# Two graph layers on one core: the edge plan in rows of one superblock a partition, spread between the batches of the relation table, and gathers that read their indices in place

## The chip, the cores and the metric

One core of one Trainium2 chip. The metric is the device time of one execution in microseconds. The median of three runs is given, and the profile is of a fourth execution.

## What is computed

12,500 nodes with 64 features, 400,000 edges sorted by destination, 16 edge types. Two layers, each with layer norm, ReLU and a residual:

```python
edge_index = jnp.stack([src, dst])
h = jnp.maximum(_layernorm(x, axis=-1), 0.0)
# layer 0: out[dst] += h[src] @ weight[edge_type]
x = x + _L0_gnn_ref(h, L0_gnn_weight, src, dst, edge_type_16)
h = jnp.maximum(_layernorm(x, axis=-1), 0.0)
# layer 1: mean of h[src] over the edges of dst, @ W_l + b_l, + h @ W_r,
#          + (edge_attr @ W_e + b_e) of the last edge of dst
x = x + _L1_gnn_ref(h, edge_index, edge_attr_16, ...)
```

## The kernel before

**Tiling.** P is 128. Nodes lie in NT = 98 tiles of 128, in NB = 14 batches of TB = 7 tiles. Edges lie in S = 125 superblocks of 128 x K, K = 25; a superblock is NG = 5 groups of G = 5 columns. A *slot* is one group, so there are SLOTS = 625 slots.

**Stage 1, loads and plan (lines 686 to 848 and 1225 to 1306).** SP loads `dst_f` (destinations, 125 partitions of 3,200, line 736), `idx` (sources in the layout partition, superblock, column, so in runs of 100 bytes, line 737), `x_sb` (rows of 256 bytes, node tile t in column t, line 738) and the weights. ACT loads `dst_i` (runs of 100 bytes), `nxt` (the destination of each column's next edge, single elements, lines 834 and 836) and the types. VectorE makes one-hots of every 16th destination in 40 steps (`hist_onehots`, line 1247), which TensorE sums to a histogram (line 1003). VectorE packs source and destination into one word (lines 1259 and 1261); ACT writes the words to DRAM (842) and copies them within DRAM to `runs`, 25,000 overlapping rows of 128 words (844 and 846). Then come checks and ends of the superblocks (lines 1275 to 1302), which end in `flag` and `s_plan`. GpSimd makes row numbers `idx * 16 + type` (701, 703). All engines are one straight line of waits here.

**Stage 2, the table.** For each batch VectorE normalises 7 tiles in six steps (`norm_step`, lines 642 to 672), TensorE turns them (1053), ACT applies ReLU (855), TensorE multiplies each tile by all 16 weights (1043, into two alternating pairs of PSUM banks), ACT and VectorE each evict one half (864, 1320) and SP stores 512 KB a tile to `rel_table` (755), 4 KB a partition. Batch n + 1 is normalised between the evictions of batch n - 1. TensorE waits for the weights before its first batch (1031, 1032).

**Stage 3, the slots.** GpSimd issues 5 indirect DMAs a slot (`gather_group`, lines 471 to 477), one row of 64 floats for each partition, with indices in `istage`. ACT copies those 5 columns of indices there (`stage_group`, 489 to 491) once the product of five slots before has freed the group (`free`), and writes the edge attributes into `msg` (893). VectorE makes one-hots of the destinations, TensorE multiplies (`product_group`, 485). The rest of the three engines' time goes to counts of edges for each pair of node tiles (lines 1069, 884, 1386 and 1387; stored by `store_counts`), which stand for layer 1's gathers and are multiplied by its features (1127). `runs_at` lists the slots after which GpSimd also gathers 128 rows of `runs` (714); its first is slot 5, and VectorE takes them from its own slot 6 on (`make_keys`, 1348). SP works through a fixed list by slot: `load_attr` at c % 5 == 1 (waits for `attr_used`), `store_counts`, `load_room`, and at slot 622 `load_piece` of the first three pieces of counts. Every instruction waits in its engine's order.

**Stage 4, the tail.** Counts come back in 106 pieces through 7 places (787) and are multiplied (1143) and evicted (1535, 1539).

## Time and profile before

| | us |
|---|---|
| median of 3 runs (lowest, highest) | 4618.67 (4602.07, 4619.43) |
| the profiled execution's own time | 4602.55 |
| its span | 4600.7 |
| busy: PE, DVE, ACT, POOL | 3003.2, 3500.4, 2121.8, 3103.8 |
| mean granted TensorE clock | 0.822 of full |

The span is that of the instructions; the execution's own time is 1.85 us more. Busy times are sums over the whole span and say little here, since the stages have different limits. The page also gives the chain of work that ended last, the costliest groups of instructions, and the DMA issues; the trace gives timelines, waits and busy time by stretch. POOL is GpSimd, DVE VectorE, ACT ScalarE, PE TensorE, SP the queue engine; a trailing q marks the queue's own instructions.

### The profile page before, as it was taken

To read this page: it belongs to the slowest core of one execution; us is meant where nothing else is said; L and a number is where in the kernel's file an instruction comes from. 1 tells how busy PE (TensorE), PEld (TensorE's weight loads), DVE (VectorE), ACT (ScalarE), POOL (GpSimd) and SP (SyncE) were. 2 spreads that over 40 slices of the span, in tenths; PEclk is the share of its full clock that TensorE was granted. 3 is DMA by queue.
4 is the path that set the end of the run, shared out by engine and by line. 5 is a ranking of instruction groups with operands and counts; after the bars stand their busy time and mean duration, and the time that the engine had idled before them with its cause. 6 is when DMAs were issued, how large, how long until landed. Compare 5 with 4: busy or idle time off the path is not lost.

```text
span 4600.7 us, 83711 instructions
## 1 busy us (share of the span) xinstructions
PE 3003.2 (65%) x23324; PEld 2426.3 (53%) x23325; DVE 3500.4 (76%) x17508; ACT 2121.8 (46%) x7155; POOL 3103.8 (67%) x3190
## 2 busy tenths in 40 slices
PE   1464555555565666565676677766777777777799
PEld 1123444444444544454565555655666666666689
DVE  5564778778788877887888888887888888888833
ACT  0243455545455554554545455454554554545400
POOL 1017777777777777777777777777777777777700
PEclk9985767767777777787787788878988989989999
DMA  9872333333323433242342433423423333332379
GB/s 101 262 307 61 116 92 116 114 110 110 101 85 109 136 120 113 92 131 76 100 142 87 126 117 91 124 74 112 121 82 111 113 94 107 109 89 76 111 286 383
DMA packets 315349, 575.64 MB, mean 125 GB/s; under 512 B 124155, under 2 KB 227259, under 8 KB 303515
## 3 DMA queue, kind: packets, MB, share of 16 engines
q1 hardware_dynamic: 135494, 443.69, 26.9%
q0 software_dynamic: 101568, 105.81, 11.4%
q10 hardware_dynamic: 77842, 20.86, 3.6%
q8 instruction: 198, 3.24, 0.3%
q14 instruction: 247, 2.02, 0.1%
HBM read 334.10 MB, written 248.81 MB: 127 GB/s over the span
## 4 chain that ended last, share of the span: by engine, by line
POOL 59%; issue 20%; PE 9%; DMA 6%; ACT 2%; DVE 2%; ACTq 1%; another core or an unknown queue 1%; POOLq 0%; SPq 0%; DVEq 0%
POOL msg L475 58%; DMA msg<-rel_table,istage 5%; PE ps L1143 4%; PE ps L1043 2%; PE ps L485 2%; ACT arena L884 2%; POOL wrel L714 1%; ACTq L846 1%; DVE onehot L1247 1%; DMA arena<-counts 1%; PE ps L1127 1%; DMA arena<-in_dst 0%; PE ps L1069 0%; DVE arena L670 0%
## 5 line engine op out<-in xcount | busy, mean ns | idle before, releaser
L475 POOL DMA_INDIRECT msg<-rel_table,istage x3125 | 3040.3, 973 | 953.7 <-issue 939.9
L884 ACT CAST arena<-ps 128x392 bf16<-128x392 f32 x3136 | 1326.5, 511 | 1945.7 <-PE ps L1069 1930.8
L485 PE MATMUL ps<-onehot,msg 128*81 128x128 f32 x6250 | 1083.5, 336 | 1124.7 <-DMA msg<-rel_table,istage 1082.3
L485 PEld LDWEIGHTS ps<-onehot,msg 128*81 128x81 f32 x6250 | 925.3, 192 | 1225.2 <-DMA msg<-rel_table,istage 1099.7
L1387 DVE TENSOR_SCALAR batch<-iota_h,wrel 128x196 bf16<-128x196 bf16 x4312 | 1248.2, 294 | 0.0
L1386 DVE TENSOR_SCALAR batch<-iota_h,wrel 128x128 bf16<-128x128 bf16 x4312 | 1173.5, 275 | 0.0
L503 DVE TENSOR_SCALAR onehot<-iota_w,arena 128x128 f32<-128x128 f32 x3125 | 684.9, 299 | 544.0 <-PE ps L485 542.6
L1069 PE MATMUL ps<-batch 128*128 128x196 bf16 x4312 | 761.6, 287 | 186.6 <-DVE batch L1387 88.9
L893 ACT ACTIVATE msg<-attr,arena 128x16 f32<-128x16 f32 x3125 | 693.6, 317 | 4.5 <-DMA attr<-in_edge_attr 4.4
L1127 PE MATMUL ps<-arena 128*128 128x192 bf16 x7238 | 690.0, 254 | 0.0
L1127 PEld LDWEIGHTS ps<-arena 128*128 128x128 bf16 x7238 | 636.6, 102 | 7.4 <-issue 0.3
L1069 PEld LDWEIGHTS ps<-batch 128*128 128x128 bf16 x4312 | 396.9, 110 | 446.1 <-DVE batch L1387 212.4
L1387 DVE TENSOR_SCALAR arena<-iota_h,wrel 128x196 bf16<-128x196 bf16 x1960 | 568.5, 294 | 0.0
L1386 DVE TENSOR_SCALAR arena<-iota_h,wrel 128x128 bf16<-128x128 bf16 x1960 | 537.8, 277 | 6.8 <-PE ps L1069 5.9
L1069 PE MATMUL ps<-arena 128*128 128x196 bf16 x1960 | 358.7, 284 | 105.7 <-ACT arena L884 49.3
L1069 PEld LDWEIGHTS ps<-arena 128*128 128x128 bf16 x1960 | 185.5, 109 | 234.2 <-issue 112.7
L1143 PE MATMUL ps<-arena 128*128 128x192 bf16 x2366 | 197.4, 246 | 4.4 <-DMA arena<-counts 3.8
L1143 PEld LDWEIGHTS ps<-arena 128*128 128x128 bf16 x2366 | 195.1, 98 | 5.8 <-issue 5.7
L1399 DVE TENSOR_TENSOR arena<-arena,ps 81x128 f32 x125 | 35.1, 281 | 200.4 <-PE ps L485 195.2
L491 ACT COPY istage<-arena 128x5 int32<-128x5 int32 x625 | 135.7, 217 | 69.9 <-PE ps L485 61.3
L708 POOL MEMSET msg<- 128x25 f32 x1 | 0.1, 140 | 221.8 <-DMA rel_table<-arena 221.8
L1535 DVE TENSOR_REDUCE batch<-ps 128x64 f32<-128x192 f32 x98 | 35.0, 357 | 114.4 <-PE ps L1143 114.4
(149 smaller groups left out, 1210.9 us busy)
## 6 DMA issues: line engine op xcount, KB each, us to landing
arena<-counts SPq DMA_DIRECT2D x458, 224.0 KB, 4.3
rel_table<-arena SPq DMA_DIRECT2D x98, 512.0 KB, 3.5
msg<-rel_table,istage POOLq DMA_INDIRECT x3125
counts<-arena SPq DMA_DIRECT2D x10, 3136.0 KB
arena<-counts SPq DMA_DIRECT2D x28, 896.0 KB, 11.9
attr<-in_edge_attr SPq DMA_DIRECT2D x125, 200.0 KB
counts<-arena SPq DMA_DIRECT2D x8, 2688.0 KB
arena<-counts SPq DMA_DIRECT2D x31, 672.0 KB, 10.8
```

Source lines behind the costliest of these rows:

```text
L475: pool.indirect_dma_start(msg[:, k, 0:D], None, table, bass.IndirectOffsetOnAxis(ap=istage[:, k:k + 1].bitcast(U32), axis=0)).then_inc(got ...
L485: mm = pe.matmul(ps[0:rows, bank, 0:WIN], msg[:, k, 0:rows], onehot[:, k, :], start=(k == 0), stop=(k == K - 1))
L491: copy(istage[:, g * G:g * G + G], slots(idx, s, g)).then_inc(ly["staged"], 1)
L503: ins = nc.vector.tensor_scalar(onehot[:, k, :], iota_w[:, :], where, None, ALU.is_equal)
L884: nc.scalar.copy(cblk[:, h, :, u * WU * WD:(u + 1) * WU * WD].rearrange("p t (w d) -> p w t d", d=WD), unit_cols(b, u).rearrange("p w (t d ...
L893: ins = nc.scalar.activation(msg[:, k, D + 1:M0], attr[:, k, :], ACT.Copy, scale=mark)
L1043: mm = pe.matmul(bank, hTs[q * D:(q + 1) * D, h, t, :], wrel_flat[q * D:(q + 1) * D, half], start=True, stop=True)
L1069: mm = pe.matmul(unit_cols(b, u)[:, w, :], oh_lo[i], oh_hi[i], start=True, stop=True)
L1127: mm = pe.matmul(mult_bank(k), weights, y3d[:, t, :], start=(t == m["t0"]), stop=(t == m["t1"] - 1))
L1143: mm = pe.matmul(tail_bank(b), places[i % PLACES].rearrange("p (t n) -> p t n", n=P)[:, t - t0, :], y3d[:, t, :], start=(t == done[b]), st ...
L1386: nc.vector.tensor_scalar(oh_lo[i], iota_h[:, 0:P], kcol[:, 1, c:c + 1], None, ALU.is_equal)
L1387: ins = nc.vector.tensor_scalar(oh_hi[i], iota_h[:, :], kcol[:, 0, c:c + 1], None, ALU.is_equal)
```

## The change

- **Layout of the plan.** Destinations, sources and types are loaded one superblock of 3,200 edges a partition (`dst_n`, `src_n`, `typ_n`, 125 partitions; the first two with 112 edges of the next superblock, so that `nxt`, `dst_f`, `dst_i`, `idx` and `typ_i` are not loaded). Row numbers, last marks and places in the window are made there and turned by TensorE into the old layout: 75 transposes in 21 turns of up to 4, each copied out by ACT (`turn_edges`, `take_turn`).
- **x for the table.** Each partition takes 98 consecutive nodes (127 partitions of 25,088 bytes, and one of 13,824); table rows are addressed to match. The tile layout is loaded again in 7 parts by SP at slots 8 to 14 for stage 3.
- **Order.** The 40 histogram steps (5 a batch) and the plan (`plan_step(n)`) are laid between the batches; only the first 5 histogram steps come before them. ACT evicts both halves of tiles 1, 3 and 5 of a batch. All batches are unrolled.
- **runs** are stored from SBUF by SP at slots 0 to 7, 16 partitions each (200 rows of 512 bytes a partition), instead of over DRAM by ACT. The first gather of them moves from slot 5 to slot 9 and waits for all these stores.
- **Gathers** wait for `free` themselves and read their index column in `idx`; `istage` is not used in this path. Waits on `staged` become waits on the landing of the gathers.

```diff
+    NAT, HALO = P * K, P - GRAIN
+    WIDE = NAT + HALO
+    HELD = NT - (NN - N)
+    ACT_ROWS = (1, 3, 5)
+    HIST_EACH = 5
+    TURN_K = 4
+    turns = [(v, k, min(k + TURN_K, K)) for v in range(3) for k in range(0, K, TURN_K)]
+    TURN_POINTS = [(n, j) for n in (2, 3) for j in range(3)] + [(4, 0), (8, 1), (8, 2)] + [
+        (n, j) for n in range(9, 13) for j in range(3)]
+    turn_at_point = {point: i for i, point in enumerate(TURN_POINTS)}
+    assert len(turns) == len(TURN_POINTS)
+    ROWS_AT, ROWS_AFTER = 7, 7
+    RUN_PARTS, X_PARTS = 8, 7
...
-        packed = rel.bitcast(I32)
...
-        nxt = sb("nxt", [P, S], I32)
...
-        t0v = table0.rearrange("(t p r) d -> p t (r d)", p=P, r=R)
+        t0v = table0.rearrange("(p t r) d -> p t (r d)", p=P, r=R)
...
+        def dve_rows(i):
+            return i // TB * (TB - len(ACT_ROWS)) + sum(t not in ACT_ROWS for t in range(i % TB))
+        def x_tiles(j):
+            return j * (NT // X_PARTS), min((j + 1) * (NT // X_PARTS), FULL)
...
-            pool.wait_ge(s_pack, 2)
-            nc.gpsimd.tensor_single_scalar(idx, idx, R, ALU.mult).then_inc(s_rowno, 1)
-            pool.wait_ge(s_rowno, 1)
-            nc.gpsimd.tensor_tensor(idx, idx, typ_i, ALU.add).then_inc(s_rowno, 1)
-            pool.wait_ge(s_rowno, 2)
-            pool.wait_ge(s_edges, 3)
...
-                    gather_group(pool, LY[0], got[0], table0, c // NG, c % NG)
+                    pool.wait_ge(LY[0]["free"], c + 1)
+                    pool.nop(nofuse=True)
+                    for k in range(c % NG * G, c % NG * G + G):
+                        pool.indirect_dma_start(
+                            msg[:, k, 0:D], None, table0,
+                            bass.IndirectOffsetOnAxis(ap=idx[:, c // NG, k:k + 1].bitcast(U32),
+                                                      axis=0)).then_inc(got[0][c % NG], 16)
                     if c == runs_at[0]:
-                        pool.wait_ge(s_runs, 32)
+                        pool.wait_ge(s_runs, (RUN_PARTS + 1) * 16)
...
-            sp.dma_start(dst_f, dst.rearrange("(p c g) -> p c g", p=FP, g=GRAIN)).then_inc(s_dstf, 16)
-            sp.dma_start(idx, edges(src)).then_inc(s_idx, 16)
-            sp.dma_start(x_sb[:, 0:FULL], xv).then_inc(s_x, 16)
+            sp.wait_ge(s_xfill, 1)
+            sp.dma_start(x_flat[0:P - 1], x[0:(P - 1) * NT].rearrange("(p t) d -> p (t d)", t=NT)).then_inc(s_x, 16)
+            sp.dma_start(x_flat[P - 1:P, 0:HELD * D], x[(P - 1) * NT:N].rearrange("(p t) d -> p (t d)", p=1)).then_inc(s_x, 16)
...
-            sp.wait_ge(s_xfill, 1)
-            sp.dma_start(x_sb[0:PART, FULL], x[FULL * P:N, :]).then_inc(s_x, 16)
...
+            sp.wait_ge(s_turned, len(turns))
...
-                    sp.wait_ge(LY[0]["staged"], SLOTS)
+                    sp.wait_ge(got[0][NG - 1], S * 16 * G)
...
+            def store_runs(j):
+                p0, p1, most = j * (P // RUN_PARTS), min((j + 1) * (P // RUN_PARTS), S - 1), NAT // GRAIN
+                part = packed_n[p0:p1]
+                sp.dma_start(runs[p0 * most:p1 * most, :].rearrange("(p r) e -> p r e", r=most),
+                             bass.AP(part.tensor, part.offset, [part.ap[0], [GRAIN, most], [1, P]])).then_inc(s_runs, 16)
...
+                    if 0 <= c < RUN_PARTS:
+                        store_runs(c)
+                    if RUN_PARTS <= c < RUN_PARTS + X_PARTS:
+                        load_x(sp, c - RUN_PARTS)
...
-            act.dma_start(dst_i, edges(dst)).then_inc(s_dst, 16)
-            act.wait_ge(s_nfill, 1)
-            act.dma_start(nxt[:, 0:S - 1], dst[K:K + (S - 1) * P * K].rearrange("(s p k) -> p s k", p=P, k=K)[:, :, 0:1]
-                          .rearrange("p s k -> p (s k)"), allow_slow_non_contiguous=True).then_inc(s_nxt, 16)
-            act.dma_start(nxt[0:P - 1, S - 1:S], dst[K + (S - 1) * P * K:E].rearrange("(p k) -> p k", k=K)[:, 0:1],
-                          allow_slow_non_contiguous=True).then_inc(s_nxt, 16)
-            act.dma_start(typ_i, edges(edge_type)).then_inc(s_typ, 16)
-            act.wait_ge(s_pack, 2)
-            act.dma_start(edges(ends), packed).then_inc(s_ends_out, 16)
-            act.wait_ge(s_ends_out, 16)
-            act.dma_start(runs[0:MAXRUN, :],
-                          bass.AP(ends.tensor, ends.offset, [[GRAIN, MAXRUN], [1, P]])).then_inc(s_runs, 16)
-            act.dma_start(runs[MAXRUN:MAXRUN + 1, :], ends[E - P:E].rearrange("(r e) -> r e", r=1)).then_inc(s_runs, 16)
+            act.wait_ge(s_nfill, 2)
+            for v, o, done_sem in ((dst, dst_n, s_dst), (src, src_n, s_idx)):
+                act.dma_start(o[0:S - 1], bass.AP(v.tensor, v.offset, [[NAT, S - 1], [1, WIDE]])).then_inc(done_sem, 16)
+                act.dma_start(o[S - 1:S, 0:NAT], v[(S - 1) * NAT:E].rearrange("(s e) -> s e", s=1)).then_inc(done_sem, 16)
+            act.dma_start(typ_n.bitcast(I32), edge_type.rearrange("(s e) -> s e", s=S)).then_inc(s_typ, 16)
...
+            def take_turn(n, j):
+                if (n, j) not in turn_at_point:
+                    return
+                i = turn_at_point[n, j]
+                v, k0, k1 = turns[i]
+                act.wait_ge(s_turn, i + 1)
+                if v > 0:
+                    act.wait_ge(s_hmm, FR // HC)
+                nc.scalar.copy((idx, last, rel)[v][:, :, k0:k1].rearrange("p s k -> p k s"),
+                               ps[:, 3, 0:(k1 - k0) * S].rearrange("p (k s) -> p k s", s=S)).then_inc(s_turned, 1)
...
+                        if t in ACT_ROWS:
+                            nc.scalar.copy(tbuf[:, t], ps[:, bank:bank + 2, :]).then_inc(FA["actout"], 1)
+                        else:
+                            nc.scalar.copy(tbuf[:, t, 0], ps[:, bank, :]).then_inc(FA["actout"], 1)
...
-                    stage_group(LY[0], 0, 0, c, act, nc.scalar.copy)
...
+            def turn_edges(n, j):
+                if (n, j) not in turn_at_point:
+                    return
+                i = turn_at_point[n, j]
+                v, k0, k1 = turns[i]
+                pe.wait_ge(s_edges, v + 1)
+                if i >= 1:
+                    pe.wait_ge(s_turned, i)
+                if i == ROWS_AFTER:
+                    pe.wait_ge(s_rowsc, 1)
+                pe.nop(nofuse=True)
+                for k in range(k0, k1):
+                    mm = pe.transpose(ps[:, 3, (k - k0) * S:(k - k0 + 1) * S], by_edge[v][:, k, :], ident[0:S, 0:S])
+                mm.then_inc(s_turn, 1)
...
+                turn_edges(n, 0)
+                if n >= 1:
+                    rel_rows(n - 1, 1 - h, n)
+                for c in range(n * HIST_EACH, min((n + 1) * HIST_EACH, FR // HC)):
+                    hist_step(c)
+            for n in range(NB):
+                table_batch(n, n % 2)
+            rel_rows(NB - 1, 1, NB)
...
-            def hist_onehots(c, q):
-                if n_from(c, 2):
-                    dve.wait_ge(s_hmm, c - 1)
-                for r, lo, hi in ((0, 0, P), (1, P, P + NP)):
-                    ins = nc.vector.tensor_tensor(
-                        hoh[:, q, :, lo:hi], iota_h[0:FP, 0:hi - lo].unsqueeze(1).broadcast_to([FP, HC, hi - lo]),
-                        fcol[:, r, bass.ds(c * HC, HC)].unsqueeze(2).broadcast_to([FP, HC, hi - lo]), ALU.is_equal)
-                ins.then_inc(s_hoh, 1)
-            hist_onehots(0, 0)
-            hist_onehots(1, 1)
-            with dve.Fori(1, FR // HC // 2) as i:
-                for q in range(2):
...
+            def hist_onehots(n):
+                for c in range(n * HIST_EACH, min((n + 1) * HIST_EACH, FR // HC)):
+                    if c >= HOHS:
...
+            def plan_step(n):
+                here, after = dst_n[:, 0:NAT], dst_n[:, 1:NAT + 1]
+                if n == 1:
+                    dve.wait_ge(s_idx, 32)
+                    dve.wait_ge(s_typ, 16)
+                    nc.vector.scalar_tensor_tensor(out=idx_n, in0=src_n[:, 0:NAT], scalar=float(R), in1=typ_n.bitcast(I32),
+                                                   op0=ALU.mult, op1=ALU.add).then_inc(s_edges, 1)
+                if n == 2:
+                    dve.wait_ge(s_edges, 1)
+                    nc.vector.tensor_single_scalar(packed_n, src_n, NODE_BITS, ALU.arith_shift_left).then_inc(s_pack, 1)
+                    dve.wait_ge(s_pack, 1)
+                    nc.vector.tensor_tensor(packed_n, packed_n, dst_n, ALU.bitwise_or).then_inc(s_pack, 1)
+                if n == 3:
+                    link(nc.vector.tensor_tensor(last_n, after, here, ALU.is_lt))
+                if n == 4:
+                    link(nc.vector.tensor_reduce(bad[0:S, 1:2], last_n, AX, ALU.max))
+                if n == 5:
+                    link(nc.vector.tensor_reduce(col[0:S, 0:1], here, AX, ALU.min))
+                if n == 6:
+                    link(nc.vector.tensor_reduce(col[0:S, 1:2], here, AX, ALU.max))
...
+                if n == 7:
+                    nc.vector.tensor_tensor(last_n, here, after, ALU.not_equal).then_inc(s_edges, 1)
+                    dve.wait_ge(s_pack, 2)
+                    dve.wait_ge(s_edges, 2)
+                    nc.vector.tensor_scalar(rel_n, here, col[0:S, 0:1], None, ALU.subtract).then_inc(s_edges, 1)
...
+            hist_onehots(0)
...
+                    if m >= 0 and t not in ACT_ROWS:
...
+            for n in range(NB):
+                plan_step(n)
+                hist_onehots(n + 1)
+                take_rows(n - 1, 1 - n % 2, n, n % 2)
...
+                if n == 0:
+                    dve.wait_ge(s_x2, (X_PARTS + 1) * 16)
```

## Rows read from the trace of the kernel before

**Rows 1.** The page: the chain that ended last, shares of the span.

```profile
POOL 59%; issue 20%; PE 9%; DMA 6%; ACT 2%; DVE 2%; ACTq 1%; another core or an unknown queue 1%; POOLq 0%; SPq 0%; DVEq 0%
```

**Rows 2.** Page, costliest groups: line, engine, form, count | busy, mean ns | idle, releaser.

```profile
L475 POOL DMA_INDIRECT msg<-rel_table,istage x3125 | 3040.3, 973 | 953.7 <-issue 939.9
...
L491 ACT COPY istage<-arena 128x5 int32<-128x5 int32 x625 | 135.7, 217 | 69.9 <-PE ps L485 61.3
```

**Rows 3.** Waits of POOL: who for whom, total us, times, longest.

```profile
POOL msg L475 <- ACT istage L491: 13.8, 41, 1.6
```

**Rows 4.** Timeline, end of the table and first gathers: start us, us, engine line, operands.

```profile
309.65 0.59 ACT L864 COPY arena<-ps 128x512 f32<-128x512 f32 x1 [0.56 <-PE ps L1043]
...
319.10 0.14 POOL L708 MEMSET msg<- 128x25 f32 x1 [221.83 <-DMA rel_table<-arena]
...
320.87 4.29 POOL L475 DMA_INDIRECT msg<-rel_table,istage  x1 [1.63 <-ACT istage L491]
```

**Rows 5.** Timeline, the first 180 us: loads, histogram, plan, first transposes.

```profile
0.78 0.40 SPq L736 DMA_DIRECT2D arena<-in_dst  x1
...
2.75 37.02 SPq L738 DMA_DIRECT2D x_sb<-in_x  x1
...
21.27 0.33 DVE L1237 TENSOR_SCALAR arena<-arena 125x200 int32<-125x200 int32 x1 [17.97 <-DMA arena<-in_dst]
...
22.41 42.45 DVE L1247 TENSOR_TENSOR onehot<-iota_h,arena 125x640 bf16<-125x640 bf16 x80
...
64.76 1.79 DVE L1259 TENSOR_SCALAR arena<-arena 128x3125 int32<-128x3125 int32 x1
...
66.59 3.42 DVE L1261 TENSOR_TENSOR arena<-arena 128x3125 int32<-128x3125 int32 x1
...
76.49 3.41 DVE L1276 TENSOR_REDUCE attr<-arena 128x125 f32<-128x3125 int32 x1
...
123.89 42.51 ACTq L846 DMA_DIRECT2D edge_runs<-edge_ends  x1
...
169.72 1.73 PE L1053 MATMUL ps<-ident,arena 128*128 128x128 f32 x7 [34.84 <-DVE arena L670]
```

**Rows 6.** Timeline, one batch of the table.

```profile
239.15 0.95 PE L1053 MATMUL ps<-ident,arena 128*128 128x128 f32 x7 [0.99 <-DVE arena L670]
...
240.04 7.51 PE L1043 MATMUL ps<-wrel,onehot 64*128 64x512 f32 x28
...
241.31 0.69 DVE L1320 COPY arena<-ps 128x512 f32<-128x512 f32 x1 [1.17 <-PE ps L1043]
241.91 0.62 DVE L652 SCALAR_TENSOR_TENSOR batch<-stat,x_sb 128x448 f32<-128x448 f32 x1
...
247.31 1.08 DVE L670 TENSOR_TENSOR arena<-batch,stat 128x896 f32<-128x896 f32 x1
```

**Rows 7.** Stretches: busy time (x instructions) by engine, PEclk, DMA share, GB/s.

```profile
200.00:300.00 100.00, 87.47 (x375) 32.95 (x373) 80.62 (x136) 55.37 (x96) 0.00 (x0) 1.00 0.98 392
...
4376.00:4420.00 44.00, 38.36 (x422) 37.98 (x423) 9.13 (x21) 4.26 (x10) 0.46 (x1) 0.88 0.42 145
...
4450.00:4500.00 50.00, 50.00 (x609) 50.00 (x607) 18.00 (x56) 0.00 (x0) 0.00 (x0) 1.00 1.03 408
```

**Rows 8.** DMA issues: operands, queue, count, KB each, us from issue to landing.

```profile
edge_runs<-edge_ends ACTq DMA_DIRECT2D x1, 12496.0 KB, 45.4
...
arena<-in_dst SPq DMA_DIRECT2D x1, 1562.5 KB
```

**Rows 9.** Timeline, last slots: staging, loads of counts, last gather, first tail product.

```profile
4350.98 0.25 ACT L491 COPY istage<-arena 128x5 int32<-128x5 int32 x1
...
4352.28 1.29 SPq L787 DMA_DIRECT2D arena<-counts  x3
...
4375.51 0.94 POOL L475 DMA_INDIRECT msg<-rel_table,istage  x1 [0.30 <-issue]
...
4392.20 1.40 PE L1143 MATMUL ps<-arena 128*128 128x192 bf16 x15
```

More of the change, by code:

```diff
@@ L76, in gnn_two_layers @@
     turn_at = [unit_slot(2 * m - 1, UB - 1) - 1 for m in range(NP)]
-    runs_at = [NG] + [unit_slot(2 * m - 2, RUNS_AT) for m in range(1, NP)]
+    runs_at = [RUN_PARTS + 1] + [unit_slot(2 * m - 2, RUNS_AT) for m in range(1, NP)]
     taken = set(turn_at) | {c + 1 for c in turn_at}
@@ L296, in gnn_two_layers @@
         s_pack = sem("s_pack")
-        s_ends_out = sem("s_ends_out")
         s_runs = sem("s_runs")
@@ L788, in load_piece @@
                              counts_of(b, t0, t1)).then_inc(cloaded[i % PLACES], 16)
+            def store_runs(j):
[3 more added lines that the diff above has]
+                             bass.AP(part.tensor, part.offset, [part.ap[0], [GRAIN, most], [1, P]])).then_inc(s_runs, 16)
+                if p1 == S - 1:
+                    part = packed_n[p1:S]
+                    sp.dma_start(runs[p1 * most:MAXRUN + 1, :].rearrange("(p r) e -> p r e", p=1),
+                                 bass.AP(part.tensor, part.offset, [part.ap[0], [GRAIN, MAXRUN + 1 - p1 * most], [1, P]])
+                                 ).then_inc(s_runs, 16)
             def load_room(i):
@@ L817, in _ @@
             with sp.Else():
+                for j in range(X_PARTS):
+                    load_x(sp, j)
                 for_steps(sp, load_attr)
@@ L872, in _ @@
             dense = is_dense(act)
-            act.wait_ge(s_rowno, 2)
-            act.wait_ge(s_edges, 3)
+            act.wait_ge(s_turned, len(turns))
             def write_unit(b, u):
                 h = b % 2
+                if u == 0 and b == 0:
+                    act.wait_ge(s_runs, (RUN_PARTS + 1) * 16)
                 if u == 0 and b >= 2:
@@ L888, in attr_group @@
             def attr_group(s, g):
+                act.wait_ge(LY[0]["free"], s * NG + (g + 1))
                 if g == 0:
@@ L998, in _, with hist_step @@
         def _(pe):
-            def hist_step(c, q, first=False, end=False):
+            def hist_step(c):
                 pe.wait_ge(s_hoh, c + 1)
                 for k in range(HC):
-                    mm = pe.matmul(ps[:, 7, 0:NP], hoh[:, q, k, 0:P], hoh[:, q, k, P:P + NP],
-                                   start=(k == 0 and first), stop=(k == HC - 1 and end))
+                    mm = pe.matmul(ps[:, 2, 0:NP], hoh[:, c % HOHS, k, 0:P], hoh[:, c % HOHS, k, P:P + NP],
+                                   start=(k == 0 and c == 0), stop=(k == HC - 1 and c == FR // HC - 1))
@@ L1005, in hist_step @@
                 mm.then_inc(s_hmm, 1)
-            HS = FR // HC
-            hist_step(0, 0, first=True)
-            hist_step(1, 1)
-            with pe.Fori(1, HS // 2 - 1) as i:
-                for q in range(2):
-                    hist_step(i * 2 + q, q)
-            hist_step(HS - 2, 0)
-            hist_step(HS - 1, 1, end=True)
-            pe.wait_ge(s_hist, 1)
-            pe.matmul(ps[0:NP, 6, 0:P], hist[:, :], ones[:, :], start=True, stop=True).then_inc(s_tot, 1)
-            pe.wait_ge(s_totc, 1)
@@ L1045, in rel_rows @@
                     mm.then_inc(FA["rows"], 1)
+                    if t == 2:
+                        turn_edges(n, 1)
+                    if t == 5:
+                        turn_edges(n, 2)
             def table_batch(n, h):
+                plan_step(n)
                 pe.wait_ge(FA["norm"], n + 1)
[L1049 to L1050 removed]
+                if n >= 1:
+                    pe.wait_ge(FA["relu"], n)
                 pe.nop(nofuse=True)
                 for t in range(TB):
[L1053 removed]
+                    mm = pe.transpose(tile_cols(0, 0, P)[:, t, :], twice[:, h, t].rearrange("p q d -> p (q d)"),
                                       ident[:, :])
                 mm.then_inc(FA["hT"], 1)
[L1056 to L1059 removed]
+                turn_edges(n, 0)
+                if n >= 1:
+                    rel_rows(n - 1, 1 - h, n)
+                for c in range(n * HIST_EACH, min((n + 1) * HIST_EACH, FR // HC)):
+                    hist_step(c)
+            for n in range(NB):
+                table_batch(n, n % 2)
+            rel_rows(NB - 1, 1, NB)
+            pe.wait_ge(s_plan, 1)
             dense = is_dense(pe)
```

252 lines of the change are left out of this document (131 added, 121 removed).

## The prediction

> **What bounds the kernel now.** I read the chain of waits first, since busy shares over the whole span mix four stages. It gives POOL 59% and "issue" 20% [rows 1]. The costliest groups say what that is: 3,125 indirect DMAs of 973 ns with 0.3 us between them [rows 2], so (3040.3 + 953.7) / 3125 = 1.278 us each and 3,994 us of a 4,601 us span, on one engine that never pauses longer. The waits of POOL show what the indices' staging costs it: 13.8 us in 41 waits [rows 3], of which 41 x 0.3 = 12.3 are the gap that stands before every gather anyway. The slots are thus bound by POOL's own time for a gather, and no other engine matters there unless it stops POOL.
>
> What is left is ahead of the first gather and behind the last. The first gather starts at 320.87, right after the last row of the table has landed (319.10) [rows 4]. Within that, the first transposes of the table start at 169.72 [rows 5], and its last tile is evicted at about 310 [rows 4]: 141.5 us of table after 169.7 us of loads and plan. The tail runs from the last gather at 4375.51 [rows 9] to 4600.7. The change works on the first 320 us.
>
> **Gathers without staging.** 625 copies of 217 ns leave ACT [rows 2], which is not the bound. POOL gains at most 13.8 - 12.3 = 1.5 us. The index column is read with the same 128 accesses; nothing in the trace prices another base address, so between -20 ns and +20 ns a gather (60 us either way) I take 0, because the gathers of the shown rows take 0.94 us whichever column of the staging tile they read [rows 9]. With the staging wait gone POOL waits for `free`, which is what ACT waited for: at the end of the slots the staging of the last slot was done at 4350.98 while POOL came to its last gather at 4375.51 [rows 9], so POOL trails its permission by 20 us and sees neither. Term: -2.
>
> **When x is there.** This decides the case. The table now starts with x and nothing of the plan except five histogram steps. The kernel before has one load with an odd number of rows: `dst_f`, 125 rows of 12,800 bytes, issued at 0.78 [rows 5]; VectorE, which waits for it, starts at 21.27. That is 1562.5 KB [rows 8] in 20.4 us, 78 GB/s, where transfers of 128 rows reach 408 GB/s [rows 7], or 408 / 16 = 25.5 GB/s for each of 16 DMA engines. My reading: whole rows are dealt in equal shares, so the number of engines must divide the number of rows. 128 gives 16, 125 gives 5 (at most 127 GB/s, and 78 beside the other loads), 124 gives 4, and 127, a prime, gives one. The new x is 127 rows of 25,088 bytes, 3.19 MB: 3.19 / 25.5 = 125 us on one engine. The new loads of destinations and sources (124 rows, 4 engines) and types (125 rows, 5) put 0.42 + 0.42 + 0.32 = 1.16 MB on each of their first engines, 46 us. They are issued in the same microsecond as x. If they meet on its engine x lands at 0.8 + 125 + 46 = 172 us, otherwise at 126. I take 172, since the load of 125 rows got 78 of 127 GB/s, so it did share its engines with the queue beside it.
>
> The Trainium skill, "DMA: Bandwidth & Descriptors", section "Why a DMA increments its semaphore by 16 and not by 1", states this as a rule: the largest number up to 16 that divides the outermost dims, taken from the lowest-numbered engines, with 127 partitions as its example of one engine. By it x lands at 172, at 126 never; no row here shows a transfer of 127 long rows.
>
> From x to the first transposes are the six steps of `norm_step`: four of 0.62, ACT 0.3, reciprocal 0.2, the last 1.08 [rows 6], 4.4 us. So 176.5 against 169.7. Term: +7. The 40 histogram steps (42.45 us) and the plan [rows 5] would have fitted into this wait, and so would all work on sources and destinations; but VectorE stands at its wait for x, and all of it is queued behind.
>
> **The table with the plan in it.** A batch took 9.4 us before: TensorE 0.95 for transposes and 7.51 for products [rows 6], VectorE 80.6 and ACT 55.4 in 100 us, and DMA share 0.98 at 392 GB/s [rows 7]. Added on VectorE, in order: five histogram steps of 42.45 / 40 = 1.06, 5.3 us a batch for n = 0 to 6; plan steps over 3,200 columns, which cost 3.5 for two inputs or a reduction and 1.8 for one input (3.42, 3.41 and 1.79 for 3,125 [rows 5]): 3.5, 5.3, 3.5, 3.5, 3.5, 4.5, 6.2 and 0.9 for n = 1 to 8. They stand ahead of the evictions of their batch. TensorE has two pairs of banks, so after two tiles it waits for VectorE: nothing covers the rest of this time. From the end of the plan step the batch needs about 8.0: VectorE's first norm step and eviction (0.62 + 0.69), five more tiles at 1.13, an eviction by ACT of 1,024 columns (twice 0.58 [rows 4]) in the chain, the last eviction. So n = 0: 9.9 (histogram and norm only); n = 1 to 7: 16.8, 18.6, 16.8, 16.8, 16.8, 17.8, 14.2; n = 8: 9. The 21 turns have four transposes each, 4 x 0.137 [rows 6], and a round trip to ACT's copy of 500 columns, about 1.2 us on TensorE when it stands between tiles; three in each of batches 9 to 12 make these 13, and those of batches 2 and 8 add 2 each. The last batch and its rows take 9.5 + 8. Sum: 9.9 + 117.8 + 9 + 4 + 52 + 17.5 = 210, with 2 for the small steps of n = 9 to 12: 212, against 141.5. Term: +70.5, with -25 (if half of VectorE's part hides) and +20 (if transposes over a stride of 100 bytes or the unrolled code cost more) as bounds. ACT has some 8 us of work in such a batch and is covered. The stores of table rows have a longer pitch in DRAM; they now need 3.67 MB in 17 us instead of 9.4, so even at half their rate they are hidden.
>
> **The stores of runs.** They leave the first part (where `runs` took 42.5 us of issue at 123.89 [rows 5], waited for by ACT's square root) and come beside slots 0 to 7: 12.8 MB in rows of 512 bytes, eight DMAs of 16 partitions. POOL comes to its first gather of runs after 50 gathers, 3.3 + 50 x (0.94 + 0.30) = 66 us from the first one [rows 4, 9], and now waits there for all stores; behind this wait are all later gathers, so it costs one for one. The same bytes took 45.4 us within DRAM [rows 8], 282 GB/s; at the 78 GB/s of the 125-row load they would take 164. From the first value (the same packet size and the same target, so the nearest) parts 0 to 5 are written by 40 us; parts 6 and 7 are issued only after slot 5's attributes, at about 45, and are there at 60 to 75. Term: +8, bounds 0 and +100. The loads of x for stage 3 (3.2 MB, needed at slot 57) and of attributes are small beside that.
>
> **The tail.** SP now waits at slot 622 for the landing of the last gathers, about 4381.6, instead of loading three pieces at 4352.28. Their first product was at 4392.20 [rows 9]; 4.5 MB take 11 us, and DMA was used at 42% up to 4420 [rows 7], so most is absorbed. Term: +2, bounds 0 and +10.
>
> **Sum.** -2 + 7 + 70.5 + 8 + 2 = +85.5 on the profiled execution's 4602.6, thus 4688. Two of the three runs shown lie 16 to 17 above that execution and one equals it, so I say **4695**. This case's own range, from its bounds, is 4640 to 4735. Chance 0.42.
>
> **Rivals.**
> *Stores through a narrow side.* If 16 neighbouring partitions are reached through a quarter of the paths, the stores run at 4 x 25.5 = 102 GB/s and take 125 us; they begin 4 us before the first gather, so POOL waits from 66 to 121 or later, 58 us instead of 8: 4745, range 4725 to 4790. It decides as soon as the stores need over 70 us, 183 GB/s. For it: 78 GB/s of the 125-row load shows that row placement can cost; against: nothing here shows it for 16 rows. Chance 0.34. The Trainium skill, "SBUF — State Buffer", section "Door 1: The DMA port swizzle", states it: partitions 0 to 15 reach 4 of 16 ports, measured 104 GB/s at 1 MiB. By that figure the stores take an estimated 123 us.
> *x spread over all engines* (faster). Then all 8 MB land in 20 us at 408 GB/s; VectorE has its first destinations by about 12, and transposes start near 27 instead of 169.7: -143 + 70.5 + 8 = -64: 4540 to 4560, or 4600 with narrow stores. It decides where x lands before about 87 us (172 less the 85 of the sum), 37 GB/s. Against it stands 78 GB/s for 125 rows. Chance 0.15.
> *VectorE's new work hides* and the table stays near 150: 4625. Against: two pairs of banks, and 80% of VectorE used already. Chance 0.09.
>
> **How the numbers follow.** A measurement here tells about 0.5%, 23 us. Faster by more: 0.12 (x spread, stores not narrow). Within: 0.10 (x spread with narrow stores 0.03, hidden work 0.07). Slower: 0.78. The range reaches up over the narrow stores and down to the edge of the spread cases, 4605 to 4775; outside are 0.12 below and some 0.06 above.
>
> **What would show it.** Right: in the changed profile VectorE's first reduction of x after a DMA wait of over 100 us; a period of 17 us in batches 1 to 6; POOL's gathers without a change in duration, one wait of POOL for the stores of runs. Wrong: a first transpose before 90 us, or a table of under 180 us. The wait of POOL at its 51st gather separates the first two cases: under 20 us or over 45.

## The result, and the profile after

The changed kernel takes 4746.59 us (median of four runs, 4742.94 to 4748.93); the kernel before, beside it on the same chip, 4613.12 (4602.07 to 4619.43). The ratio is 1.0286 with a 95% interval of 1.0262 to 1.0311. The profiled execution took 4742.94 with a span of 4741.1, 140.4 more than the span before. The direction and the range were right, the case forecast as likeliest was not: 4746.6 lies beyond that case's own end of 4735 and on the rival of the narrow stores (4745). The forecast of 4695 was 82 us of loss, and 133.5 were measured.

The waits of POOL in the changed kernel (who waited for whom: total us, times, longest), which answer to [rows 3]:

```profile
POOL msg L744 <- issue: 926.4, 3031, 3.0
POOL msg L729 <- DMA rel_table<-arena: 394.1, 1, 394.1
POOL wrel L735 <- DMA edge_runs<-arena: 63.0, 1, 63.0
POOL msg L744 <- PE ps L512: 28.6, 94, 0.3
```

One new wait stands there, 63.0 us at the first gather of `runs`. The gathers themselves, from the page's costliest groups, are as in [rows 2]:

```profile
L744 POOL DMA_INDIRECT msg<-rel_table,arena x3125 | 3044.9, 974 | 955.1 <-issue 926.4
```

The start, VectorE's timeline (against [rows 5]): beside twelve short instructions, this is all that VectorE did in the first 177 us.

```profile
61.43 0.33 DVE L1317 TENSOR_SCALAR arena<-arena 125x200 int32<-125x200 int32 x1 [55.81 <-DMA arena<-in_dst]
...
62.56 5.39 DVE L1328 TENSOR_TENSOR arena<-iota_h,arena 125x640 bf16<-125x640 bf16 x10
176.91 0.62 DVE L674 TENSOR_REDUCE stat<-x_sb 128x7 f32<-128x448 f32 x1 [108.97 <-DMA x_sb<-in_x]
```

And stretches of the same execution (start and end, length, busy time of PE, PEld, DVE, ACT and POOL with their instructions, granted clock, DMA share, GB/s; the columns of [rows 7]). The first is the load of x by itself, the next two are batches of the table, and the last is the time in which POOL waits for the stores of `runs`.

```profile
100.00:160.00 60.00, 0.00 (x0) 0.00 (x0) 0.00 (x0) 0.00 (x0) 0.00 (x0) 1.00 0.06 27
...
210.00:231.00 21.00, 11.91 (x62) 5.25 (x61) 16.05 (x22) 8.78 (x12) 0.00 (x0) 0.76 0.44 178
...
332.60:373.00 40.40, 39.17 (x189) 18.45 (x188) 24.97 (x44) 34.25 (x47) 0.00 (x0) 1.00 0.84 342
...
461.00:530.00 69.00, 7.27 (x30) 6.15 (x30) 0.00 (x0) 5.07 (x25) 4.80 (x6) 0.50 0.70 110
```

A DMA share of 0.06 is one engine of sixteen, at 27 GB/s: the x of 127 rows. The next two stretches show the table in its two forms: with the plan in it TensorE works 11.9 of 21 us at a mean clock of 0.76; without it, from 332.6 on, 39.2 of 40.4 at 1.00.

**Where the 140.4 us are.** Each line compares the same two events in the profiles. The last eviction of the table is VectorE's, first in the kernel before and then in the changed one:

```profile
310.51 0.69 DVE L1320 COPY arena<-ps 128x512 f32<-128x512 f32 x1 [0.17 <-PE ps L1043]
...
389.17 0.69 DVE L1415 COPY arena<-ps 128x512 f32<-128x512 f32 x1 [1.50 <-PE ps L1112]
```

| stretch | before | after | difference | predicted |
|---|---|---|---|---|
| start to first transposes of x | 169.72 | 182.80 | +13.1 | +7 |
| to the end of that eviction (311.20, 389.86) | 141.5 | 207.1 | +65.6 | +70.5 |
| to the first gather (320.87, 399.09) | 9.67 | 9.23 | -0.4 | 0 |
| POOL's wait for `runs` | 0 | 63.0 | +63.0 | +8 |
| rest, first to last gather (last at 4375.51, 4520.83) | 4054.6 | 4058.7 | +4.1 | -2 |
| last gather to the end | 225.2 | 220.3 | -4.9 | +2 |
| sum | 4600.7 | 4741.1 | +140.4 | +85.5 |

Of the 55 us by which the sum was short, the stores of `runs` are 55. The errors of the other terms are -6.9 to +6.1 us and add up to nothing, which is luck.

### The profile page after: what moved, and what is told of

It is laid out like the page before. It is cut to its first block, busy times and chain, and to the rows that moved or that the text cites. A ratio compares the mean times of both kernels' runs of the same rounds, so it can differ in the third digit from the quotient of the medians.

```text
span 4741.1 us, 82631 instructions
## 1 busy us (share of the span) xinstructions
PE 3016.7 (64%) x23397; PEld 2436.7 (51%) x23398; DVE 3484.4 (73%) x17468; ACT 2094.7 (44%) x6549; POOL 3094.3 (65%) x3188
## 4 chain that ended last, share of the span: by engine, by line
POOL 53%; issue 17%; PE 13%; DMA 7%; another core or an unknown queue 3%; DVE 3%; SPq 2%; ACT 1%; POOLq 0%; ACTq 0%; DVEq 0%
POOL msg L744 52%; DMA msg<-rel_table,arena 6%; PE ps L512 5%; PE ps L1222 4%; PE ps L1112 2%; SPq L821 2%; PE ps L1206 1%; POOL wrel L735 1%; DVE arena L1328 1%; PE ps L1148 1%; DMA arena<-counts 1%; DMA edge_runs<-arena 1%; SPq L788 0%; DVE batch L1477 0%
## 5 line engine op out<-in xcount | busy, mean ns | idle before, releaser
L744 POOL DMA_INDIRECT msg<-rel_table,arena x3125 | 3044.9, 974 | 955.1 <-issue 926.4
L951 ACT ACTIVATE msg<-attr,arena 128x16 f32<-128x16 f32 x3125 | 679.6, 316 | 94.8 <-DMA attr<-in_edge_attr 52.9
L1112 PE MATMUL ps<-wrel,onehot 64*128 64x512 f32 x392 | 115.7, 708 | 50.9 <-DVE arena L1415 48.0
L1127 PE MATMUL ps<-ident,arena 128*128 128x128 f32 x98 | 15.1, 299 | 189.4 <-DVE arena L697 189.4
```

Of the source, the lines that this page charges most:

```text
L744: pool.indirect_dma_start(msg[:, k, 0:D], None, table0, bass.IndirectOffsetOnAxis(ap=idx[:, c // NG, k:k + 1].bitcast(U32), axis=0)).then_ ...
L951: ins = nc.scalar.activation(msg[:, k, D + 1:M0], attr[:, k, :], ACT.Copy, scale=mark)
L1112: mm = pe.matmul(bank, hTs[q * D:(q + 1) * D, h, t, :], wrel_flat[q * D:(q + 1) * D, half], start=True, stop=True)
```

## The experiments

Where a kernel was timed once, its time is compared with that of the changed kernel's profile (4742.94); where it was timed several times beside the kernel before, the ratio to that kernel is given with its 95% interval. The time of the slots differs from execution to execution for no cause that I know: in the thirteen profiles with the new gathers the stretch from the first gather to the last, less POOL's wait for `runs`, takes 4058.7 to 4081.3 us. A single time is thus good to some 20 us, and I read each step from the events around it.

### x on more engines

The load of x, one of 127 partitions, is cut in two; nothing else is edited.

```diff
-sp.dma_start(x_flat[0:P - 1], ...)
+sp.dma_start(x_flat[0:112], ...)
+sp.dma_start(x_flat[112:127], ...)
```

> The changed kernel with one edit: the load of x in 127 rows is made in two, 112 rows and 15 rows. Theory (the number of DMA engines divides the number of rows, so 127 rows ran on one): 16 and 15 engines carry it, each engine's share of x falls from 3.19 MB to about 0.2 MB, and VectorE's first reduction of x moves from 176.9 us to about 33, where the five histogram steps end; the first batches then wait some 10 us for sources and types, whose 4 and 5 engines still carry 1.16 MB each (until about 58). First gather at about 265 instead of 399, time about 4607. Rival (long rows of 25 KB or the two queues side by side are slow, whatever the number of rows): x stays beyond 150 us and the time within 10 us of 4743.

Measured: 4635.4, a first gather at 291.71 instead of 399.09, 107.4 us earlier. VectorE no longer waits for x at all: its first reduction follows the histogram steps (48.20 to 53.5) directly. It comes at 53.5 and not at 33, since VectorE has its destinations only at 47.07. And the gain was to be some 28 us more. VectorE's and TensorE's timelines say why:

```profile
47.07 0.33 DVE L1318 TENSOR_SCALAR arena<-arena 125x200 int32<-125x200 int32 x1 [41.45 <-DMA arena<-in_dst]
...
53.50 0.61 DVE L674 TENSOR_REDUCE stat<-x_sb 128x7 f32<-128x448 f32 x1
...
79.84 1.73 PE L1128 MATMUL ps<-ident,arena 128*128 128x128 f32 x7 [79.84 <-DMA bl<-in_L_gnn_b_l]
```

VectorE's part was ready at 59 (its last norm step ran 58.04 to 59.13). TensorE waited for the last of the weights, which stand behind x in SP's queue. SP's own rows of this kernel show it held there:

```profile
3.86 0.40 SPq L764 DMA_DIRECT2D x_sb<-in_x  x1
...
17.32 48.61 SPq L770 DMA_DIRECT2D wcomb<-in_L_gnn_W_l  x1
65.98 3.88 SPq L771 DMA_DIRECT2D wcomb<-in_L_gnn_W_r  x1
...
70.75 2.06 SPq L774 DMA_DIRECT2D bl<-in_L_gnn_b_l  x1
```

The issue of one 16 KB weight took 48.6 us. From 20 to 50 us the DMA share was 0.38, some six of the sixteen engines: the loads of destinations, of sources and of types were still under way. The same cut at another place, 124 partitions and 3:

> The same load in 124 rows and 3 rows, a middle dose. Theory: 4 engines, so the first of them carries 31 rows of x (0.78 MB), three small remainders and 1.16 MB of the other loads, together 1.98 MB at 25.5 GB/s = 78 us: VectorE's first reduction of x at about 82 us, first gather at about 305, time about 4648. Rival (no dependence on the number of rows): as the changed kernel, reduction at 177.

Measured: 4674.34. Destinations arrive at 77.01, the reduction of x at 83.44, and TensorE starts at 112.46, again behind the weights. 124 rows, a multiple of 4, are 32.6 us worse at the first transposes than 112 rows, a multiple of 16, with the same bytes in the same number of loads; the first gather is at 323.85, 32.1 later. When x itself landed the trace does not date here: VectorE reads it right behind its histogram steps, which began when the destinations came. The number of rows decides, and the first cause of the late start is settled. My two forecasts were low by 28 and 26 us, each time because I left out what is late next: the weights.

### The stores of runs

The same 12.8 MB stand in the same partitions of SBUF; what is edited is which of them one store takes. First by columns: each of eight stores takes 25 rows of every one of 112 partitions, and one more store takes the 12 partitions that are left.

```diff
-part = packed_n[p0:p1]                  # 16 neighbours, 200 rows of each
+part = packed_n[0:112]                  # 112 partitions, 25 rows of each
```

> The changed kernel with the stores of runs cut by columns instead of by partitions: eight stores of 112 partitions x 25 rows of 512 bytes, one of the 12 partitions left and the last one; as many bytes, as many packets, the same 16 engines. Theory (16 neighbouring partitions are reached through a quarter of the paths): 11.5 MB go at 280 GB/s in 41 us and the 12 partitions take 15, so all are there by about 55 us after the first gather and the wait of POOL falls from 63 us to under 5: about 4682. Rival (packets of 512 bytes out of SBUF, or their issue on SP, are the limit): the wait stays above 50 us.

Measured: 4691.04. POOL does not wait for `runs` at all. The total is 9 us over the 4682 that were expected; the slots took 4071.6 us instead of 4058.7. Then with wider groups of neighbours, in one kernel four parts of 32 partitions and in another two of 64:

```diff
-p0, p1, most = j * (P // RUN_PARTS), min((j + 1) * (P // RUN_PARTS), S - 1), NAT // GRAIN
+p0, p1, most = j * 32, min((j + 1) * 32, S - 1), NAT // GRAIN
```

> The changed kernel, with the stores of runs in 4 parts of 32 neighbouring partitions (slots 0 to 3) instead of 8 of 16; nothing else. Theory A (a group of 16 neighbours reaches a quarter of the paths, 32 reach half): the stores run at up to 204 GB/s instead of 96, 12.8 MB take about 65 to 75 us from 394, so they are there at 460 to 470, when GpSimd arrives (464): its wait falls from 63 to 0 to 12 us, total 4683 to 4695. Rival B (the queue or the 512 byte packets set the rate, not the width; both forms divide by 16): the wait stays near 63 and the total near 4743. Rival C (a fixed cost of each store, which column parts of 112 partitions also had): the wait would halve, total about 4712.

> The changed kernel, with the stores of runs in 2 parts, partitions 0 to 63 and 64 to 123 (slots 0 and 1). Theory A (paths are reached by position, and partition p + 32 lies on the path of p): 64 neighbours are no wider than 32, but the two parts lie on different halves and may run side by side: the wait of GpSimd is 0 to 12, total 4680 to 4695. If they run one after the other, as 4 parts of 32. Rival B (a rate set by the queue or by 512 byte packets): wait near 63, total near 4743. The second part has 60 partitions, so it may be dealt to 15 or 12 engines; a wait of 5 to 20 more is put to that.

Measured: waits of 7.5 and 6.1 us; times 4704.99 and 4691.63. Both waits are what was expected; the first time is 10 above its range, and its slots took longer otherwise (4076.9 from first to last gather less the wait, against 4058.7). These forms also have fewer and larger stores, which a rival could claim. So last the clean one: eight stores of the same size at the same slots, and only other partitions in each. (Their rows in DRAM, one stretch of 1.6 MB a store before, now lie apart; in the parts of 32 they are one stretch, so that this is not what helps.)

```diff
-part = packed_n[p0:p1]
+part = packed_n[j:S - 1:RUN_PARTS]      # j, j + 8, j + 16, ...
```

> The changed kernel with the 8 stores of runs as they are in size and slot, but each takes every eighth partition (j, j + 8, ...: 16 or 15 of them) instead of 16 neighbours. Theory A (the place of the partitions sets the rate): the store runs at twice 96 GB/s or more, it is there when GpSimd comes, wait 0 to 15, total 4680 to 4697. Rival B (16 partitions a store are too few, wherever they lie, or the waits of SP's queue between 8 stores cost the time): wait 45 to 63, total 4725 to 4745.

Measured: 4685.56, a wait of 6.4. POOL's wait in this kernel:

```profile
POOL wrel L735 <- DMA edge_runs<-arena: 6.4, 1, 6.4
```

The stretches of the stores beside the gathers say how fast each form went. First this kernel:

```profile
402.00:461.00 59.00, 19.39 (x80) 16.42 (x80) 5.86 (x27) 8.80 (x40) 44.68 (x48) 0.53 0.90 213
```

the changed kernel in the same stretch:

```profile
406.00:461.00 55.00, 16.16 (x70) 13.71 (x70) 5.68 (x26) 5.51 (x25) 41.59 (x45) 0.53 0.81 135
```

the four parts of 32:

```profile
408.00:461.00 53.00, 19.38 (x80) 16.42 (x80) 5.63 (x26) 5.51 (x25) 40.20 (x43) 0.50 0.90 212
```

the two parts of 64:

```profile
400.00:461.00 61.00, 19.38 (x80) 16.42 (x80) 7.37 (x35) 6.28 (x31) 46.67 (x48) 0.50 0.89 211
```

and the stores by columns, the last third of this time:

```profile
440.00:461.00 21.00, 8.20 (x34) 7.09 (x35) 0.00 (x0) 3.30 (x15) 16.04 (x17) 0.50 1.05 282
```

All of these count gathers and attributes in too. Sixteen neighbours reach 135 GB/s (110 once the gathers stop, at 461), sixteen partitions spread over SBUF 213, 32 neighbours 212, 64 neighbours no more than that, 211. Neither the packets (512 bytes in all), nor the number of stores, nor the number of partitions in one holds the stores at the narrow rate, but the partitions' place; the theory of the narrow side is shown. By columns the rate is 282 with all DMA engines busy (a DMA share of 1.05; from 449.6 on loads of x are counted in too), as much as the copy within DRAM had; whether the packets of 512 bytes set this upper limit was not tried. The Trainium skill, "SBUF — State Buffer", section "Door 1: The DMA port swizzle", has this as a rule: partitions 0 to 15 reach 4 ports of 16, 32 neighbours 8, and 64 no more than 32. The traces agree in all three, as far as rates tell that count other traffic in; the kernel's 12.8 MB in the 133 us from 393.5 to about 527 are 96 GB/s, beside the 104 that this page of the Trainium skill gives. By this rule of the Trainium skill a stride of 8 also reaches 8 ports, as the 213 beside the 212 of 32 neighbours bears out.

What holds POOL in the narrow form is not the whole cost. SP's list, in the changed kernel:

```profile
405.88 65.38 SPq L821 DMA_DIRECT2D edge_runs<-arena  x5
471.30 14.00 SPq L788 DMA_DIRECT2D attr<-in_edge_attr  x1
485.35 14.30 SPq L821 DMA_DIRECT2D edge_runs<-arena  x2
499.70 14.00 SPq L825 DMA_DIRECT2D edge_runs<-arena  x1
```

Each issue takes 13 to 14 us; with every eighth partition the same five take 33.30, 6.7 each, so the time of the issue goes with the rate of the stores. ACT waits 42.19 us for the attributes in between (its row at 490.45). All of it is over before POOL goes on at 527.18, so I count nothing more for it.

### The table and the histogram

All 40 histogram steps ahead of VectorE's wait for x (and TensorE's sums ahead of its wait for the weights), in an otherwise unedited changed kernel:

```diff
-hist_onehots(0)
+for n in range(-(-(FR // HC) // HIST_EACH)):
+    hist_onehots(n)
 dve.wait_ge(s_x, 32)
```

> The changed kernel with all 40 histogram steps ahead of VectorE's wait for x, and their products ahead of TensorE's wait for the weights, where both are idle. Theory (work of VectorE between the batches is covered by nothing, as TensorE stands after two tiles): seven times 5.4 us leave the table and nothing is added ahead of x; first gather 38 us earlier, at about 361, time about 4705. Rival (TensorE's products, 8 us a batch, cover most of it): less than 15 us are gained.

Measured: 4700.14, 42.8 less, with x 2.1 us earlier (174.81) and the first gather 42.4 earlier (356.67).

```profile
180.70 1.73 PE L1129 MATMUL ps<-ident,arena 128*128 128x128 f32 x7 [77.42 <-DVE arena L697]
...
330.53 0.98 PE L1129 MATMUL ps<-ident,arena 128*128 128x128 f32 x7
```

From the first to the last transposes the table takes 149.8 us (180.70 to 330.53) instead of 190.5 (182.80 to 373.27): 40.6 us for 35 steps that occupy VectorE for 37.7 (seven groups of 5.38) and TensorE, whose sums moved with them, for 5.6 (seven of 0.80). At most 2.7 us of the histogram were hidden between the batches, which ends the rival of the hidden work for this part; and in the idle wait for x the histogram was free. What is left, 149.8 against 125.8 in the kernel before (169.72 to 295.56), is 24.0 us for the plan steps and the turns together. They were not moved, and what each of them costs is not shown.

### Gathers without staging

The kernel before with this part alone:

```diff
-gather_group(pool, LY[0], got[0], table0, c // NG, c % NG)
+pool.wait_ge(LY[0]["free"], c + 1)
+for k in range(...):
+    pool.indirect_dma_start(msg[:, k, 0:D], None, table0, bass.IndirectOffsetOnAxis(ap=idx[:, c // NG, k:k + 1] ...
...
-stage_group(LY[0], s, s, g, act, nc.scalar.copy)
```

> The kernel before with one part of the change alone: gathers wait for the free group themselves and read their index column in place, no staging copies on ACT. My term is -2 us of about 4613, so a ratio of 0.9995, same. Rival (the gather reads its indices slower or faster from the big array): 20 ns a gather either way, 60 us, ratio 0.987 or 1.013; the mean gather then is 953 or 993 ns instead of 973.

Measured: 4602.52 against 4607.32, ratio 0.9995 (0.998 to 1.001). POOL's waits of 13.8 for ACT are gone, and 34.4 us of the same 0.3 us gaps are put down to TensorE's `free` instead:

```profile
POOL msg L723 <- issue: 919.3, 3012, 1.6
...
POOL msg L723 <- PE ps L485: 34.4, 113, 0.3
```

919.3 + 34.4 = 953.7, the 953.7 of [rows 2]. The staging cost nothing.

### Both repairs, and beyond

> The changed kernel with both repairs: x loaded as 112 and 15 partitions, and runs stored in 8 column parts of 112 partitions. The two gains measured alone against the changed kernel were 107.5 (4635.4) and 51.9 us (4691.0). Theory: they lie at different places (before the table, after slot 8) and add up: 4742.9 - 107.5 - 51.9 = 4583.5, 0.7% under the kernel before. Rival: the stores of runs meet the attributes in both and only the sum of POOL's wait (54.8 in the first) can go: 4580. Rival: GpSimd, no longer held at slot 8, runs into the loads of x for stage 3 and pays 10 to 20 us back: 4600.

Measured: 4586.29, ratio 0.9936 (0.9915 to 0.9958) against the kernel before. The two gains add up, as the theory had it (4583.5); the first rival (4580) is too near to be told from it.

Then also the loads of destinations, sources and types, cut at partition 112:

```diff
-act.dma_start(o[0:S - 1], ...)
+act.dma_start(o[0:112], ...)
+act.dma_start(o[112:S - 1], ...)
```

> As x_wide_and_runs_by_columns, and the loads of destinations, sources and types split at partition 112 as well. Theory (the first 30 us are bound by how few engines carry these loads): destinations were there at 47.1 and the weights, which TensorE waits for ahead of its first transposes, at 79.8; with all loads on 14 to 16 engines 8 MB at 300 to 400 GB/s are in by 27 to 35 us, and the first transposes start at 35 to 45: 35 to 45 us less than the one before, 4540 to 4550. Rival: the loads' many queue entries hold the weights, which stay last on SP's queue: transposes at 60, 4565.

Measured: 4541.90, ratio 0.9856 (0.9805 to 0.9907). Destinations are there at 29.47 instead of 47.70; the first transposes come at 48.28, still after `bl`, and the first gather at 258.38. Stretches of this kernel show how the loads run with no narrow one among them:

```profile
0.00:20.00 20.00, 0.00 (x0) 0.01 (x1) 4.01 (x10) 0.00 (x0) 1.23 (x13) 1.00 0.77 203
20.00:40.00 20.00, 0.00 (x0) 0.00 (x0) 8.81 (x17) 1.42 (x2) 0.00 (x0) 1.00 1.02 200
```

All DMA engines are now busy, and yet they move 200 GB/s, half of what the table's stores of 4 KB a row reach in [rows 7]. I had counted on 300 to 400. The weights ahead of x:

> As all_plan_loads_wide, with SP's loads of the seven weights ahead of x. Theory: TensorE then waits for VectorE's first norm steps and not for the weights; if x itself lands at about 30 to 35 us the first transposes come at 36 to 42, 0 to 15 us before those of all_plan_loads_wide. Rival: the 2,048 pieces of 256 bytes of the relation weights take 12 us of queue ahead of x and x comes 12 us later: a loss of up to 12.

Measured: 4550.69, ratio 0.9872 (0.9818 to 0.9926), not distinguished from the one before. TensorE is free of the weights, but x comes at 43.17 and the first transposes at 49.06; the first gather is 6.0 us later. The rival was right: a loss of up to 12. VectorE now idles 21.63 us ahead of x, and this can be filled:

```diff
-hist_onehots(0)
+for n in range(5):
+    hist_onehots(n)
```

> As weights_ahead_of_x, with 25 of the 40 histogram steps instead of 5 ahead of VectorE's wait for x, which there was idle from 21.5 to 43.2. Theory: 20 steps of 1.08 (21.6 us) fill the idle time, the first transposes stay at 49 to 51, and four batches become 5.3 us shorter each: 4550.7 - 20 = 4531, 11 under all_plan_loads_wide. Rival: what TensorE and ACT have to do in these batches shows instead, half of it is gained: 4541.

VectorE's timeline of this kernel:

```profile
16.46 26.56 DVE L1340 TENSOR_TENSOR arena<-iota_h,arena 125x640 bf16<-125x640 bf16 x50
42.95 0.61 DVE L674 TENSOR_REDUCE stat<-x_sb 128x7 f32<-128x448 f32 x1
```

Twenty more steps fill the gap to within 0.2 us, the first transposes come at 48.83 and the first gather at 240.11, 24.2 earlier than in weights_ahead_of_x and 80.8 earlier than in the kernel before. The time is 4535.78 (4519.81 to 4553.33), ratio 0.9838 (0.9794 to 0.9881), the best of all, though its interval overlaps that of all_plan_loads_wide. The times do not tell the theory (4531) from the rival (4541); the first gather does, since 24.2 us are the whole gain and not half. The profiled execution had long slots (4081.3 us from first to last gather; all_plan_loads_wide had 4060.8).

## Why the prediction was right or wrong

**When x is there: the mechanism right, 6 us short.** One engine moved x at 27 GB/s, and VectorE had x at 176.9, not 172: SP first waited for VectorE's fill of the last rows (2.4 us) and issued x at 3.86. To the first transposes it then took 5.9 us instead of 4.4, since ACT first loads its table (1.28 us):

```profile
176.91 0.62 DVE L674 TENSOR_REDUCE stat<-x_sb 128x7 f32<-128x448 f32 x1 [108.97 <-DMA x_sb<-in_x]
...
179.59 1.28 ACT L710 ACT_TABLE_LOAD   x1 [179.59 <-DVE stat L688]
...
181.22 0.20 DVE L691 RECIPROCAL stat<-stat 128x7 f32<-128x7 f32 x1 [1.71 <-ACT stat L710]
```

The cut at 112 rows is what shows the cause: it took 107 us away.

**The table: +65.6 for +70.5, by two errors of opposite sign.** Predicted and measured (from transposes to transposes): batch 0 9.9 and 9.4; batches 1 to 7, with the 2 for turns, 119.8 and 129.2; batch 8, likewise, 11 and 11.2; batches 9 to 12, with the 2 for small steps, 54 and 40.7; the last with its rows 17.5 and 16.6. *The turns* cost less than the 1.2 us each that I gave them: batches 9 to 12, three turns each, take 10.2 instead of 13, and TensorE does four transposes in 0.71. What the new split of the evictions gives back in these batches was not measured apart. *The batches with the plan* take 1.3 more each than I worked out, 9.4 in all, and I had left out two things. One is four turns: the sum has 2 us for those of batch 2, but three more stand in batch 3 and one in batch 4, 4.8 us by my own price. The other is TensorE's clock. TensorE's timeline of batch 2, and of a batch without such a pause:

```profile
210.80 1.99 PE L1112 MATMUL ps<-wrel,onehot 64*128 64x512 f32 x8
221.62 2.08 PE L1112 MATMUL ps<-wrel,onehot 64*128 64x512 f32 x4 [8.83 <-DVE arena L1415]
223.63 1.10 PE L1097 MATMUL ps<-ident,arena 125*128 125x125 f32 x4
224.66 2.86 PE L1112 MATMUL ps<-wrel,onehot 64*128 64x512 f32 x8
...
339.94 1.13 PE L1112 MATMUL ps<-wrel,onehot 64*128 64x512 f32 x4 [0.25 <-ACT arena L913]
341.00 0.72 PE L1097 MATMUL ps<-ident,arena 125*128 125x125 f32 x4
```

After 8.8 us of waiting four products take 2.08 us instead of 1.13, and four transposes 1.10 instead of 0.72. The granted clock of these rows, and of the rows at the end of the same batch:

```profile
221.60:223.60 2.00, 1.98 (x4) 0.53 (x4) 1.03 (x2) 0.00 (x0) 0.00 (x0) 0.50 0.63 260
...
227.80:231.00 3.20, 3.20 (x30) 1.57 (x31) 2.00 (x4) 2.65 (x5) 0.00 (x0) 1.00 0.79 323
```

The first stretch is at the lower of the two levels, 1.2 GHz, the second at 2.4. Over the three rows behind the pause that is 6.0 us in place of 3.8 (1.13 + 0.72 + 1.99), 2.2 us. If each of the seven batches paid this in full it would be 15 us, more than they are over together with the turns; how much of it is in the path is open. I took TensorE's durations from a stretch in which it hardly paused and its clock was 1.00 [rows 7]; the change opens pauses of 7 to 9 us, and I kept the durations.

**The stores of runs: the step that failed.** The prediction had the rate from "the first value (the same packet size and the same target, so the nearest)", a copy within DRAM at 282 GB/s, and from it a wait of 8. The stores had 96 GB/s, and the wait was 63.0. The row was near in packets and target and far in the one thing that counted, the source: sixteen neighbouring partitions. The rival had the mechanism, its wait (58), and its time (4745 for 4746.6); it decided at a rate under 183 GB/s, and the stores had 96. With 0.34 against 0.42 the rival was weighed too low: 78 GB/s of the 125-row load was the only row of a transfer with few engines or places behind it, and the DRAM copy says nothing on SBUF at all. The case's own range did not carry its own bounds either: the term had +100 as its upper bound, yet the case ended at 4735, 40 us above its centre. That the stated range of 4605 to 4775 held is owed to the rival, for which it was widened.

**Gathers and tail.** The term of the staging, -2, stands within 0.2% of nothing (0.998 to 1.001). The mean gather is 974 ns after 973. The tail was to take 2 us more and took 4.9 less. All executions without staging have 218.6 to 221.8 from last gather to the end, the one profile of the kernel before 225.2. Whether the later loads of counts help, or that one profile was long there, is open.

**The rivals.** x spread over all engines did not come true as the change stands. Its price, 4540 to 4560, counted on all 8 MB being spread: with x alone wide, and wide stores, the kernel takes 4586; with the plan's loads wide too, 4542. The hidden work of VectorE is excluded by the histogram's experiment for the histogram, and a table of 207 us instead of the 150 of this rival excludes it for the whole.

## What to carry to other kernels

Choose the number of partitions of a transfer so that 16 divides it, and their place by how far they spread: 112 and 15 instead of 127 partitions took 107 us off, every eighth partition instead of sixteen neighbours 57 us. When a load is repaired, ask at once who waits for what stands behind it in the same queue. Work that is laid "between" batches of a stage whose pace an engine already sets is not hidden; its place is where that engine waits, and work put ahead of a wait is free as long as it fits.

## What the runs showed of the hardware

- One late weight: with x in 112 and 15 rows, SP spent 48.6 us on the issue of a 16 KB load, at a DMA share of 0.38 from 20 to 50 us. With the plan's loads wide too, the same issue took 24.2 us, and ahead of x (weights_ahead_of_x) 1.1. Loads that keep only a few engines busy still held back a small one behind them.
- Four products of 64 x 512 took 2.08 us after a pause of 8.8 us and 1.13 without one; the granted clock was 0.50 in the first case and 1.00 in the second (from 332.6 on, with pauses of some 0.3 us).
- Loads of rows of 12.8 to 25 KB ran at 200 GB/s with the DMA share at 1.02 (20 to 40 us of all_plan_loads_wide), and at 211 with a share of 0.98 in weights_ahead_of_x, where the weights' small pieces were issued before them. The table's stores with 4 KB a row ran at 377 GB/s with a share of 0.92 (321 to 333 us of the changed kernel). What halves the loads was not tried.
